# Attention stage of one transformer block: column-tiled products in 6 groups per four units instead of 14, reciprocals of 16 columns, VectorE's sums placed later

## The chip, the core and the metric

One core of one Trainium2 chip runs the whole program. Its engines work in parallel and wait for each other with semaphores: TensorE (PE, with its weight loads PEld), VectorE (DVE), ScalarE (ACT), GpSimd (POOL) and SyncE (SP), which here only starts transfers. The metric is the device time of one execution in microseconds (us).

## What is computed

A block of attention and a mixture of experts on x of 4 x 2048 x 512. Only the attention part and the shared expert run in the stage that changes:

```python
qkv = x @ Wqkv                       # x after a layer norm; 16 heads of 32
k, v = _compress(k, ...), _compress(v, ...)   # 2048 keys become 512, one null key is put ahead
dots = jnp.einsum('bhid,bhjd->bhij', q, k) * d ** (-0.5)
dots = jnp.where(mask, mask_value, dots)      # query i sees compressed key j if i >= 4j + 3
attn = jax.nn.softmax(dots, axis=-1)
out = jnp.einsum('bhij,bhjd->bhid', attn, v)
...
shared = jax.nn.silu(xf @ sh_gate_w) * (xf @ sh_up_w) @ sh_down_w
```

The block's output adds x, a Fourier transform of `out @ W_out + b_out`, `shared` and the routed experts. These other parts run in stages of their own, before and after.

## The kernel before

The program has stages one after the other: stage A (layer norm, projections, compression, routing), stage B (attention, shared expert, tables of the routing), then the routed experts and the transforms. The change touches only `stage_b`.

Stage B has NU = 64 units. A unit u is 512 queries (QC) of one batch for 4 heads (HPC), DH = 32 rows each. n = u % 4 (NCH = 4) says which quarter of the sequence it is: it sees n "past" blocks of 128 keys in full and one "diagonal" block under a mask. Each unit is cut into 12 slots k = 0..11 (SLOTS), written out in the same way on every engine. The slots are the order of the work; nothing but semaphores ties the engines together.

On PE a slot has six matmuls of the shared expert (`gate_up` in even units and the first four slots of odd ones, else `down`), then in slots 0 to 7 two `scores(u + 1, ...)` into the two banks `ps_s`, then the turned scores `scores_t` of this unit into the two banks `ps_t`, and last the column-tiled products. These use the array as four column tiles of 32, one for each head: `values` sums probabilities times values into `ps_o`, one call for each key block, and `denominators` sums the probabilities into `ps_d` with a matrix of ones. A call is four matmuls in the program and eight in the trace. I call calls that stand side by side with no other matmul between them a group. `pv_slots` puts the diagonal block in slot 6 and past block kt in slot 7 + 2 kt; `denominators` stands in slot 7 for n = 0 and otherwise in slot 0 of the next unit. For n = 0, 1, 2, 3 that is 2, 3, 4 and 5 groups, 14 in four units.

On DVE a slot has one or two steps of the shared expert (`gate_out`, `up_out`, `split_h`, `down_out`), in slot 1 `normalise(u - 1)`, in slots 2 to 5 a quarter each of the reciprocals of `den` (`invert`), in slots 0 to 7 two `row_max(u + 1, ...)`, which read `ps_s` and give the bank back, in slot 8 `negate`, and in slots 6, 8 and 10 the sums of the probabilities (`add_past`, for the n past blocks). `scores(i)` waits until `row_max(i - 2)` is done.

ACT takes the exponents of `ps_t` (`exponent`, `null_exponent`), the tanh of the gate and the rounded copies. POOL masks the diagonal block (`mask_diagonal`), scatters the routing table with single-column indirect DMAs (`scatter`, 10 or 11 in a unit while there are any) and multiplies `o` by the reciprocals (`finish`). `normalise(u)` waits for `finish(u - 1)` (`att_ready`). SP loads q, keys, values, x and its transpose, and stores `att` (`store_att`).

Of the kernel before, what the change touches and what calls it, by code (L numbers as in the profile page):

```python
# [11 lines left out]
ALU = mybir.AluOpType  # L12
# [3 lines left out]
P = 128  # L16
BATCH, SEQ, DIM = 4, 2048, 512
TOK = BATCH * SEQ
# [740 lines left out]
def stage_b(nc, t, early):  # L759
    ctx = ExitStack()  # L760
    with ctx:
# [14 lines left out]
        den = sb("den", [P, QC])  # L776
        o = sb("o", [P, QC])
# [60 lines left out]
        rden_ready = sem("rden_ready")  # L838
# [52 lines left out]

        def pv_slots(n, k):
            if k == 6:
                return [n]
            return [kt for kt in range(n) if 7 + 2 * kt == k]
# [29 lines left out]
        def _(sp):  # L925
# [85 lines left out]
            for u in range(NU):  # L1011
# [16 lines left out]
                if u:  # L1028
                    store_att(u - 1)
# [7 lines left out]
                if u in (NU // 2 - 2, NU // 2 - 1):  # L1037
                    load_raw(2 * u - NU + 12)
                    load_raw(2 * u - NU + 13)
            store_x(2 * NSTEP - 1)  # L1040
# [7 lines left out]
        def _(pool):  # L1048
            pool.iota(tokens[:, :], pattern=[[P, NTILE]], base=0, channel_multiplier=1).then_inc(tokens_ready, 1)

            def finish(u):

                pool.wait_ge(rden_ready, QTC * (u + 1))
                pool.wait_ge(od_emptied, u + 1)
                if u >= 2:
                    pool.wait_ge(att_out[u % 2], 16 * (u // 2))
                pool.tensor_tensor(att[u % 2][:, :], o[:, :], den[:, :], ALU.mult).then_inc(att_ready, 1)
# [14 lines left out]
            for u in range(NU):  # L1072
                mask_diagonal(u)
                g, part = (u - 1) // GU_UNITS - 1, (u - 1) % GU_UNITS
                mine = range(part * 4 * TOPK // GU_UNITS, (part + 1) * 4 * TOPK // GU_UNITS) if 0 <= g < NG else range(0)
                for i in mine[:4]:
                    scatter(g, i)
                if u:
                    finish(u - 1)
                for i in mine[4:]:  # L1080
                    scatter(g, i)
# [5 lines left out]
        def _(act):  # L1087
# [55 lines left out]

            split_w(0)
            max_rows(0)
            for u in range(NU):
                s, gate = steps(u)
                n = u % NCH
                for k in range(SLOTS):
# [18 lines left out]
                    for kt, h in t_slots(n, k):  # L1168
                        exponent(u, kt, h)
                    if u == 0 and k in (1, 3, 7):  # L1170
                        split_w((1, 3, 7).index(k) + 1)
# [8 lines left out]
        def _(dve):  # L1180
# [45 lines left out]
            def normalise(u):  # L1226
# [4 lines left out]
                if u:  # L1231
                    dve.wait_ge(att_ready, u)
                dve.tensor_tensor(den[:, :], ps_d[:, :], p_null[:, :], ALU.add).then_inc(den_ready, 1)
# [3 lines left out]
            def invert(u, i):  # L1237
                dve.wait_ge(den_ready, u + 1)
                part = den[:, i * P:(i + 1) * P]
                dve.reciprocal(part, part).then_inc(rden_ready, 1)  # L1240
# [102 lines left out]
            for u in range(NU):  # L1343
                s, gate = steps(u)
                for k in range(SLOTS):
# [30 lines left out]
                    if k == 1 and u:  # L1376
                        normalise(u - 1)
                    if 2 <= k < QTC + 2 and u:
                        invert(u - 1, k - 2)
# [14 lines left out]
                    if k in (6, 8, 10) and (k - 6) // 2 < u % NCH:  # L1394
                        add_past(u, (k - 6) // 2)
# [5 lines left out]
            normalise(NU - 1)  # L1401
            for i in range(QTC):
                invert(NU - 1, i)

        @block.tensor
        def _(pe):
# [64 lines left out]

            def gate_up(s, j, a, part):
# [47 lines left out]
            for u in range(NU):  # L1520
                s, gate = steps(u)
                n = u % NCH
                for k in range(SLOTS):
# [11 lines left out]
                    for kt in pv_slots(n, k):  # L1535
                        values(u, kt)
                    if k == 7 and n == 0:
                        denominators(u)
                    if k == 0 and u and (u - 1) % NCH:
                        denominators(u - 1)  # L1540
# [4 lines left out]
            denominators(NU - 1)  # L1545
# [767 lines left out]
def internal(nc):  # L2313

    def d(name, shape, dt=F32):
        return nc.dram_tensor(f"mid_{name}", shape, dt, kind="Internal").ap()
# [6 lines left out]
        attT=d("attT", (DC, P, TOK)), passed=nc.alloc_semaphore("passed"))  # L2323
# [81 lines left out]
```

## Time and profile before

| | |
|---|---|
| median of 3 runs | 5415.87 us (5412.05 to 5418.78) |
| the profiled execution's span, first to last instruction | 5418.5 us |
| PE busy | 5303.0 us, 98% |
| DVE busy | 3828.9 us, 71% |
| ACT busy | 2615.1 us, 48% |
| POOL busy | 3028.9 us, 56% |
| stage B | from about 710 to 2450 us of the span |

The execution that was profiled took what its span says; what lies around the span is not told apart, and the span is 2.6 us above the median of the runs. A share of busy time is a mean over stages with different limits. PE's matmuls are pipelined and their durations overlap, so that a busy PE may still lose time: what a matmul costs is read from the start of one to the start of the next.

### The profile page before, as it was taken

What the parts mean: (1) busy time and instruction counts of PE and PEld (TensorE: products, weight loads), DVE (VectorE), ACT (ScalarE), POOL (GpSimd) and SP (SyncE); (2) the same over time, 40 slices, a digit from 0 to 9 for tenths busy, and PEclk for the clock granted to TensorE, in tenths of its full rate; (3) what the DMA queues carried; (4) which work ended last, traced back from release to release, by engine and by line L of the source; (5) the groups of instructions that cost most, each with busy time, mean ns of one, the idle gap of its engine ahead of it and who ended that gap; (6) DMA issues with size and microseconds to landing.
All of it is one profiled execution on the core that took longest, in us unless ns stands there. A gap on an engine that the chain in (4) does not pass through costs nothing. (4 is left out here: it accounts for less than half of the span.)

```text
span 5418.5 us, 102292 instructions
## 1 busy us (share of the span) xinstructions
PE 5303.0 (98%) x32880; PEld 4440.9 (82%) x32880; DVE 3828.9 (71%) x7311; ACT 2615.1 (48%) x3833; POOL 3028.9 (56%) x2716
## 2 busy tenths in 40 slices
PE   8999989999999999998999999999999999999999
PEld 6888866766666667667999999989999999999786
DVE  6666667778787877775676666766667666666664
ACT  3333333333343333335666666666666666666410
POOL 1222215666666665115777777777777777777514
PEclk9999989999999999998999999999999999999999
DMA  7777764444454444435676677767787676676748
GB/s 239 248 242 255 250 173 129 133 134 119 136 148 135 119 141 118 134 98 119 134 158 112 134 170 150 163 132 167 158 227 158 135 164 129 134 156 113 178 154 289
DMA packets 500414, 864.75 MB, mean 160 GB/s; under 512 B 64388, under 2 KB 165493, under 8 KB 497694
## 3 DMA queue, kind: packets, MB, share of 16 engines
q1 hardware_dynamic: 356014, 567.12, 33.2%
q0 software_dynamic: 140928, 292.13, 29.5%
q10 hardware_dynamic: 3312, 3.47, 0.3%
q8 instruction: 88, 1.44, 0.1%
q14 instruction: 72, 0.59, 0.0%
HBM read 498.49 MB, written 330.47 MB: 153 GB/s over the span
## 5 line engine op out<-in xcount | busy, mean ns | idle before, releaser
L1754 POOL DMA_INDIRECT mid_base<-e_rows,e_ox x556 | 1160.3, 2087 | 372.5 <-POOL e_ox L1749 239.5
L1865 DVE TENSOR_TENSOR e_wgu_lo<-e_wgu,e_wgu_hi 128x2048 fp32r<-128x2048 f32 x278 | 637.5, 2293 | 806.4 <-ACT e_wgu_hi L1788 676.6
L1742 POOL DMA_INDIRECT e_xg<-mid_xn,e_ix x556 | 625.5, 1125 | 336.4 <-POOL e_ix L1739 226.4
L1801 ACT CAST e_xT_hi<-e_ps_t 128x512 fp32r<-128x512 f32 x556 | 299.1, 590 | 929.8 <-PE e_ps_t L1931 929.8
L1069 POOL DMA_INDIRECT mid_ids<-b_pairs,b_cell x512 | 614.3, 1200 | 141.8 <-issue 141.0
L1944 PE MATMUL e_ps_g<-e_xT_hi,e_wgu_hi 128*128 128x256 f32 x2224 | 652.9, 294 | 1.7 <-issue 1.7
L1944 PE MATMUL e_ps_g<-e_xT_lo,e_wgu_hi 128*128 128x256 f32 x2224 | 630.0, 283 | 0.0
L1944 PE MATMUL e_ps_g<-e_xT_hi,e_wgu_lo 128*128 128x256 f32 x2224 | 629.7, 283 | 0.0
L1944 PE MATMUL e_ps_u<-e_xT_hi,e_wgu_hi 128*128 128x256 f32 x2224 | 629.4, 283 | 0.0
L1944 PE MATMUL e_ps_u<-e_xT_lo,e_wgu_hi 128*128 128x256 f32 x2224 | 629.4, 283 | 0.0
L1944 PE MATMUL e_ps_u<-e_xT_hi,e_wgu_lo 128*128 128x256 f32 x2224 | 629.4, 283 | 0.0
L1197 DVE CUSTOM_DVE_ANT_0 b_ps_s<-b_ps_s,ab_mask,ab_s_null 128x32 f32<-128x32 f32 (+15 forms) x1024 | 460.3, 490 | 130.0 <-PE b_ps_s L1417 123.7
L1788 ACT CAST e_wgu_hi<-e_wgu 128x2048 fp32r<-128x2048 f32 x278 | 531.4, 1912 | 23.1 <-DMA e_wgu<-in_up_w 23.1
L1062 POOL TENSOR_SCALAR_AFFINE_SELECT b_p_diag<-b_p_diag 128x512 f32<-128x512 f32 x256 | 160.2, 650 | 537.4 <-ACT b_p_diag L1120 537.4
L1956 PE MATMUL e_ps_y<-e_wd_hi,e_hT_hi 128*128 128x512 f32 x1112 | 436.2, 392 | 0.0
L1956 PE MATMUL e_ps_y<-e_wd_lo,e_hT_hi 128*128 128x512 f32 x1112 | 436.0, 392 | 0.0
L1956 PE MATMUL e_ps_y<-e_wd_hi,e_hT_lo 128*128 128x512 f32 x1112 | 433.6, 390 | 0.0
L1944 PEld LDWEIGHTS e_ps_g<-e_xT_hi,e_wgu_hi 128*128 128x128 f32 x2224 | 426.4, 192 | 2.1 <-issue 2.1
L1944 PEld LDWEIGHTS e_ps_g<-e_xT_lo,e_wgu_hi 128*128 128x128 f32 x2224 | 427.9, 192 | 0.0
L1944 PEld LDWEIGHTS e_ps_u<-e_xT_lo,e_wgu_hi 128*128 128x128 f32 x2224 | 427.0, 192 | 0.0
L1944 PEld LDWEIGHTS e_ps_u<-e_xT_hi,e_wgu_lo 128*128 128x128 f32 x2224 | 427.0, 192 | 0.0
L1944 PEld LDWEIGHTS e_ps_g<-e_xT_hi,e_wgu_lo 128*128 128x128 f32 x2224 | 427.0, 192 | 0.0
(286 smaller groups left out, 13368.0 us busy)
## 6 DMA issues: line engine op xcount, KB each, us to landing
b_xT_hi<-mid_xT_hi SPq DMA_DIRECT2D x32, 1024.0 KB
b_xT_lo<-mid_xT_lo SPq DMA_DIRECT2D x32, 1024.0 KB
mid_base<-b_x SPq DMA_DIRECT2D x32, 1024.0 KB
e_wgu<-in_gate_w SPq DMA_DIRECT2D x62, 512.0 KB
e_wgu<-in_up_w SPq DMA_DIRECT2D x62, 512.0 KB
e_wd<-in_down_w SPq DMA_DIRECT2D x62, 512.0 KB
ec_cell<-mid_base SPq DMA_DIRECT2D x88, 256.0 KB, 4.9
ab_q<-mid_q_hi SPq DMA_DIRECT2D x82, 256.0 KB, 4.0
```

The costliest lines, as they stand in the source:

```text
L1062: pool.affine_select(p_diag[:, h, :], p_diag[:, h, :], [[1, QC]], ALU.is_ge, 0.0, base=1 - CF, channel_multiplier=-CF).then_inc(masked, 1)
L1069: pool.indirect_dma_start(t["ids"], bass.IndirectOffsetOnAxis(ap=cell[r][:, i:i + 1], axis=0), pairs[r][:, i, :], None).then_inc(scattered ...
L1197: dve.tensor_tensor_reduce(S[:, 0:w_], S[:, 0:w_], mask[:, NC - w_:NC], 1.0, null_of(u)[:, qt, h:h + 1], ALU.add, ALU.max, mx[:, qt, h:h + ...
L1742: pool.indirect_dma_start(xg[s][:, i, :], None, t["xn"], bass.IndirectOffsetOnAxis(ap=ix[s][:, i:i + 1], axis=0))\
L1754: pool.indirect_dma_start(t[f"base{i}"], bass.IndirectOffsetOnAxis(ap=ox[s][:, i:i + 1], axis=0), rows[s][:, i, :], None, compute_op=ALU.a ...
L1788: act.copy(wgu_hi[s][:, :], wgu[s][:, :]).then_inc(gu_hi_ready, 1)
L1801: act.copy(xT_hi[s][:, i * DC // 2 * RB:(i + 1) * DC // 2 * RB], ps_t[i][:, :]).then_inc(xT_hi_ready, 1)
L1865: dve.tensor_tensor(wgu_lo[s][:, :], wgu[s][:, :], wgu_hi[s][:, :].bitcast(F32), ALU.subtract)\
L1944: last = pe.matmul(dst[s][:, h * RB:(h + 1) * RB], w[s][:, w0:w0 + P], x[s][:, x0:x0 + RB], start=k == 0 and n == 0, stop=k == DC - 1 and ...
L1956: last = pe.matmul(ps_y[i][:, :], x[s][:, h0:h0 + P], w[s][:, h * DIM:(h + 1) * DIM], start=h == 0 and n == 0, stop=h == HC - 1 and n == 2)
```

## The change

`TILED` is a table that says for each n in which slot which `values` calls stand; `denominators` follows the last of them. The key SLOTS (12) stands for slot 0 of the next unit. The groups are now 1 for n = 0 (slot 7), 1 for n = 1 (slot 11), 2 for n = 2 (slot 11, and `denominators` alone in slot 0 of the next unit) and 2 for n = 3 (slot 6, and slot 0 of the next unit): 6 in four units. The number of calls is the same.

The four reciprocals of 128 x 128 on DVE become one of 128 x 16. Four rows of `den` (one for each head; the 32 rows of a head are equal) are spread over 128 partitions by a DMA (`turn_den`), inverted (`invert`), stored to DRAM (`store_rden`) and read back with each row repeated 32 times (`spread_rden`). ACT issues all three. The last unit keeps four reciprocals. `normalise` moves to slot 2 in units with n = 0, `invert` stands in slot 4 (5 for n = 0), and the sums go by the table `ADDS`. POOL issues 8 scatters ahead of `finish` in place of 4, and SP issues `store_att` behind its loads.

```diff
@@ -776,2 +776,4 @@
         den = sb("den", [P, QC])
+        den16 = sb("den16", [P, QC // DH])
+        rden = sb("rden", [P, QC])
         o = sb("o", [P, QC])
...
@@ -891,6 +896,8 @@
 
+        TILED = {0: {7: [0]}, 1: {11: [1, 0]}, 2: {11: [2, 0, 1], SLOTS: []}, 3: {6: [3, 0], SLOTS: [1, 2]}}
+
         def pv_slots(n, k):
-            if k == 6:
-                return [n]
-            return [kt for kt in range(n) if 7 + 2 * kt == k]
+            return TILED[n].get(k, [])
+
+        ADDS = {0: (), 1: (7,), 2: (8, 9), 3: (6, 8, 10)}
 
@@ -1027,4 +1034,2 @@
                     load_group(u // GU_UNITS + 1)
-                if u:
-                    store_att(u - 1)
                 if gate and s:
@@ -1039,2 +1044,4 @@
                     load_raw(2 * u - NU + 13)
+                if u:
+                    store_att(u - 1)
             store_x(2 * NSTEP - 1)
@@ -1052,3 +1059,3 @@
 
-                pool.wait_ge(rden_ready, QTC * (u + 1))
+                pool.wait_ge(rden_in, 16 * (u + 1))
                 pool.wait_ge(od_emptied, u + 1)
@@ -1056,3 +1063,3 @@
                     pool.wait_ge(att_out[u % 2], 16 * (u // 2))
-                pool.tensor_tensor(att[u % 2][:, :], o[:, :], den[:, :], ALU.mult).then_inc(att_ready, 1)
+                pool.tensor_tensor(att[u % 2][:, :], o[:, :], rden[:, :], ALU.mult).then_inc(att_ready, 1)
 
@@ -1075,3 +1082,3 @@
                 mine = range(part * 4 * TOPK // GU_UNITS, (part + 1) * 4 * TOPK // GU_UNITS) if 0 <= g < NG else range(0)
-                for i in mine[:4]:
+                for i in mine[:8]:
                     scatter(g, i)
@@ -1079,3 +1086,3 @@
                     finish(u - 1)
-                for i in mine[4:]:
+                for i in mine[8:]:
                     scatter(g, i)
@@ -1142,2 +1149,17 @@
                 act.copy(hT_hi[:, j, :], hT[:, :]).then_inc(h_hi_ready, 1)
+
+            def turn_den(u):
+
+                act.wait_ge(den_ready, u + 1)
+                act.dma_start(den16[:, :], den[0:P:DH, :].rearrange("h (j c) -> h j c", j=DH)).then_inc(den16_in, 16)
+
+            def store_rden(u):
+                act.wait_ge(den16_ready, u + 1)
+                act.dma_start(t["rden"].rearrange("h (j c) -> (h j) c", j=DH), den16[:, :]).then_inc(rden_out, 16)
+
+            def spread_rden(u):
+                act.wait_ge(rden_out, 16 * (u + 1))
+                if u:
+                    act.wait_ge(att_ready, u)
+                act.dma_start(rden[:, :], t["rden"][:, None, :].broadcast_to([HPC, DH, QC])).then_inc(rden_in, 16)
 
@@ -1169,2 +1191,8 @@
                         exponent(u, kt, h)
+                    if u and k == (3 if u % NCH == 0 else 2):
+                        turn_den(u - 1)
+                    if u and k == (6 if u % NCH == 0 else 5):
+                        store_rden(u - 1)
+                    if u and k == (8 if u % NCH == 0 else 7):
+                        spread_rden(u - 1)
                     if u == 0 and k in (1, 3, 7):
@@ -1232,2 +1260,3 @@
                     dve.wait_ge(att_ready, u)
+                    dve.wait_ge(den16_in, 16 * u)
                 dve.tensor_tensor(den[:, :], ps_d[:, :], p_null[:, :], ALU.add).then_inc(den_ready, 1)
@@ -1236,6 +1265,5 @@
 
-            def invert(u, i):
-                dve.wait_ge(den_ready, u + 1)
-                part = den[:, i * P:(i + 1) * P]
-                dve.reciprocal(part, part).then_inc(rden_ready, 1)
+            def invert(u):
+                dve.wait_ge(den16_in, 16 * (u + 1))
+                dve.reciprocal(den16[:, :], den16[:, :]).then_inc(den16_ready, 1)
 
@@ -1375,6 +1403,6 @@
                             down_out(s, k // 2 - 3 if k > 7 else 0)
-                    if k == 1 and u:
+                    if u and k == (2 if u % NCH == 0 else 1):
                         normalise(u - 1)
-                    if 2 <= k < QTC + 2 and u:
-                        invert(u - 1, k - 2)
+                    if u and k == (5 if u % NCH == 0 else 4):
+                        invert(u - 1)
                     if u + 1 < NU:
@@ -1393,4 +1421,4 @@
                         early.place_heads(dve, kc[1]).then_inc(heads_placed, 1)
-                    if k in (6, 8, 10) and (k - 6) // 2 < u % NCH:
-                        add_past(u, (k - 6) // 2)
+                    if k in ADDS[u % NCH]:
+                        add_past(u, ADDS[u % NCH].index(k))
                     g, part = (u - 1) // GU_UNITS, (u - 1) % GU_UNITS
@@ -1401,4 +1429,5 @@
             normalise(NU - 1)
+            dve.wait_ge(den_ready, NU)
             for i in range(QTC):
-                invert(NU - 1, i)
+                dve.reciprocal(rden[:, i * P:(i + 1) * P], den[:, i * P:(i + 1) * P]).then_inc(rden_in, 16 // QTC)
 
@@ -1470,2 +1499,9 @@
                 last.then_inc(d_filled, 1)
+
+            def tiled(u, k):
+                n = u % NCH
+                for kt in pv_slots(n, k):
+                    values(u, kt)
+                if k == max(TILED[n]):
+                    denominators(u)
 
@@ -1534,8 +1570,5 @@
                         scores_t(u, kt, h)
-                    for kt in pv_slots(n, k):
-                        values(u, kt)
-                    if k == 7 and n == 0:
-                        denominators(u)
-                    if k == 0 and u and (u - 1) % NCH:
-                        denominators(u - 1)
+                    if k == 0 and u:
+                        tiled(u - 1, SLOTS)
+                    tiled(u, k)
                     if k == 10:
@@ -1544,3 +1577,3 @@
                         scores_null(u)
-            denominators(NU - 1)
+            tiled(NU - 1, SLOTS)
 
...
```

PE, a unit with n = 0, from the scores of slot 6 to those of slot 7 and the groups that follow them (b_ps_f is the shared expert, b_ps_s the scores, b_ps_o `values`, b_ps_d `denominators`). Before:

```order
L1417 MATMUL b_ps_s<-ab_kc,ab_q 128x256 x2
L1456 MATMUL b_ps_o<-b_p_diag,ab_vc 32x512 x4
L1490 MATMUL b_ps_f<-b_xT_hi,b_wgu_hi 128x512
L1490 MATMUL b_ps_f<-b_xT_lo,b_wgu_hi 128x512
L1490 MATMUL b_ps_f<-b_xT_hi,b_wgu_lo 128x512
L1490 MATMUL b_ps_f<-b_xT_hi,b_wgu_hi 128x512
L1490 MATMUL b_ps_f<-b_xT_lo,b_wgu_hi 128x512
L1490 MATMUL b_ps_f<-b_xT_hi,b_wgu_lo 128x512
L1417 MATMUL b_ps_s<-ab_kc,ab_q 128x256 x2
L1469 MATMUL b_ps_d<-b_p_diag,b_ones 32x512 x4
L1490 MATMUL b_ps_f<-b_xT_hi,b_wgu_hi 128x512
```

And of the change:

```order
L1446 MATMUL b_ps_s<-ab_kc,ab_q 128x256 x2
L1526 MATMUL b_ps_f<-b_xT_hi,b_wgu_hi 128x512
L1526 MATMUL b_ps_f<-b_xT_lo,b_wgu_hi 128x512
L1526 MATMUL b_ps_f<-b_xT_hi,b_wgu_lo 128x512
L1526 MATMUL b_ps_f<-b_xT_hi,b_wgu_hi 128x512
L1526 MATMUL b_ps_f<-b_xT_lo,b_wgu_hi 128x512
L1526 MATMUL b_ps_f<-b_xT_hi,b_wgu_lo 128x512
L1446 MATMUL b_ps_s<-ab_kc,ab_q 128x256 x2
L1485 MATMUL b_ps_o<-b_p_diag,ab_vc 32x512 x4
L1498 MATMUL b_ps_d<-b_p_diag,b_ones 32x512 x4
L1526 MATMUL b_ps_f<-b_xT_hi,b_wgu_hi 128x512
```

What were two groups, with the six matmuls of the shared expert between them, is one group of both calls.

DVE, in a unit with n = 1, slots 3 and 4 (L1197 before and L1225 now is `row_max`; b_gated and b_hT are the shared expert; b_slot is the routing). Before:

```order
L1245 SCALAR_TENSOR_TENSOR b_gated<-b_gated,b_ps_f 128x512
L1240 RECIPROCAL b_den<-b_den 128x128
L1197 ISA b_ps_s,b_mx<-b_ps_s,ab_mask,ab_s_null 128x320
L1197 ISA b_mx 128x1
L1197 ISA b_ps_s,b_mx<-b_ps_s,ab_mask,ab_s_null 128x320
L1197 ISA b_mx 128x1
L1283 TENSOR_TENSOR b_slot<-b_slot,b_pos 128x256
L1253 SCALAR_TENSOR_TENSOR b_hT<-b_gated,b_ps_f 128x512
L1240 RECIPROCAL b_den<-b_den 128x128
```

And of the change:

```order
L1273 SCALAR_TENSOR_TENSOR b_gated<-b_gated,b_ps_f 128x512
L1225 ISA b_ps_s,b_mx<-b_ps_s,ab_mask,ab_s_null 128x320
L1225 ISA b_mx 128x1
L1225 ISA b_ps_s,b_mx<-b_ps_s,ab_mask,ab_s_null 128x320
L1225 ISA b_mx 128x1
L1311 TENSOR_TENSOR b_slot<-b_slot,b_pos 128x256
L1281 SCALAR_TENSOR_TENSOR b_hT<-b_gated,b_ps_f 128x512
L1268 RECIPROCAL b_den<-b_den 128x16
```

The two reciprocals of 128 columns of these slots are gone, and one of 16 columns stands in slot 4.

ACT, in a unit with n = 2, from its first exponents to the null exponent's copy (b_p_diag and b_p_past are exponents, b_gated the tanh, b_hT_hi a rounded copy). Before:

```order
L1120 ACTIVATE b_p_diag<-b_ps_t 128x512 x4
L1136 ACTIVATE b_gated<-b_ps_f 128x512
L1120 ACTIVATE b_p_past<-b_ps_t 128x512 x4
L1142 CAST b_hT_hi<-b_hT 128x512
L1120 ACTIVATE b_p_past<-b_ps_t 128x512 x2
L1136 ACTIVATE b_gated<-b_ps_f 128x512
L1120 ACTIVATE b_p_past<-b_ps_t 128x512 x2
L1142 CAST b_hT_hi<-b_hT 128x512
```

And of the change:

```order
L1127 ACTIVATE b_p_diag<-b_ps_t 128x512 x4
L1143 ACTIVATE b_gated<-b_ps_f 128x512
L1127 ACTIVATE b_p_past<-b_ps_t 128x512
L1154 DMA b_den<-b_den 128x1x16
L1127 ACTIVATE b_p_past<-b_ps_t 128x512 x3
L1149 CAST b_hT_hi<-b_hT 128x512
L1127 ACTIVATE b_p_past<-b_ps_t 128x512 x2
L1158 DMA mid_rden<-b_den 128x16
L1143 ACTIVATE b_gated<-b_ps_f 128x512
L1127 ACTIVATE b_p_past<-b_ps_t 128x512 x2
L1164 DMA b_rden<-mid_rden 128x1x512
L1149 CAST b_hT_hi<-b_hT 128x512
```

Three DMA issues stand among ACT's instructions; each has its wait for a semaphore ahead of it.

## Rows read from the trace of the kernel before

**Rows 1.** The page's part 1: busy us (share of the span) xinstructions.

```profile
PE 5303.0 (98%) x32880; PEld 4440.9 (82%) x32880; DVE 3828.9 (71%) x7311; ACT 2615.1 (48%) x3833; POOL 3028.9 (56%) x2716
```

**Rows 2.** By windows: PE, PEld, DVE, ACT, POOL busy, granted clock, DMA share, GB/s.

```profile
750.00:2448.00 1698.00, 1684.30 (x8246) 1171.22 (x8245) 1345.65 (x3473) 649.16 (x1020) 855.23 (x827) 1.00 0.44 127
```

**Rows 3.** Timeline of PE, `denominators` alone; start us, us, engine, line, out<-in.

```profile
1609.68 0.40 PE L1417 MATMUL b_ps_s<-ab_kc,ab_q 96*128 96x256 f32 x2
1610.02 1.07 PE L1469 MATMUL b_ps_d<-b_p_diag,b_ones 128*32 128x512 f32 x8
1611.01 0.50 PE L1490 MATMUL b_ps_f<-b_xT_hi,b_wgu_hi 128*128 128x512 f32 x1
1611.35 0.39 PE L1490 MATMUL b_ps_f<-b_xT_lo,b_wgu_hi 128*128 128x512 f32 x1
1611.57 0.39 PE L1490 MATMUL b_ps_f<-b_xT_hi,b_wgu_lo 128*128 128x512 f32 x1
```

**Rows 4.** Timeline, the stage's end, two calls side by side on PE.

```profile
2445.84 1.06 PE L1456 MATMUL b_ps_o<-b_p_past,b_vc 128*32 128x512 f32 x8
...
2446.72 1.04 PE L1469 MATMUL b_ps_d<-b_p_sum,b_ones 128*32 128x512 f32 x8
```

**Rows 5.** Timeline of PE, ends of slots 5 (n = 1, 2, 0).

```profile
1628.79 0.40 PE L1512 MATMUL b_ps_f<-b_wd_hi,b_hT_lo 128*128 128x512 f32 x1
1629.03 0.79 PE L1417 MATMUL b_ps_s<-ab_kc,ab_q 96*128 96x352 f32 x2
1630.02 0.47 PE L1512 MATMUL b_ps_f<-b_wd_hi,b_hT_hi 128*128 128x512 f32 x1 [0.21 <-DVE b_hT_lo L1257]
...
1656.12 0.49 PE L1417 MATMUL b_ps_s<-ab_kc,b_q 96*128 96x480 f32 x1 [0.24 <-DVE b_mx L1197]
1656.76 0.48 PE L1417 MATMUL b_ps_s<-ab_kc,b_q 96*128 96x480 f32 x1
...
1711.50 0.39 PE L1490 MATMUL b_ps_f<-b_xT_hi,b_wgu_lo 128*128 128x512 f32 x1
1711.99 0.74 PE L1417 MATMUL b_ps_s<-b_kc,ab_q 96*128 96x224 f32 x2
1712.57 0.40 PE L1490 MATMUL b_ps_f<-b_xT_hi,b_wgu_hi 128*128 128x512 f32 x1
```

**Rows 6.** Waits in stage B: who <- whom: us in total, times, longest.

```profile
PEld b_ps_s L1417 <- DVE b_mx L1197: 40.0, 102, 2.3
PE b_ps_s L1417 <- DVE b_mx L1197: 5.6, 19, 1.9
```

**Rows 7.** The view by lines, DVE and POOL in the same window.

```profile
L1240 DVE RECIPROCAL b_den<-b_den 128x128 f32<-128x128 f32 x252 | 238.3, 946 | 0.0
L1069 POOL DMA_INDIRECT mid_ids<-b_pairs,b_cell x512 | 614.3, 1200 | 141.8 <-issue 141.0
L1057 POOL TENSOR_TENSOR b_att<-b_o,b_den 128x512 f32<-128x512 f32 x63 | 83.2, 1320 | 187.7 <-DVE b_den L1240 171.1 <-issue 16.5
```

**Rows 8.** Timeline of DVE, a short reciprocal in stage A.

```profile
221.24 0.18 DVE L584 RECIPROCAL a_winv<-a_wsum 128x4 f32<-128x4 f32 x1
```

**Rows 9.** DMA issues: KB, us to landing; last row: q loads (L933).

```profile
mid_w<-a_w SPq DMA_DIRECT2D x16, 16.0 KB, 2.0
...
DMA to landing us min/median/max: 3.2/4.2/6.3
```

**Rows 10.** Timeline, a unit with n = 3, slots 2 to 5.

```profile
1678.86 0.60 ACT L1120 ACTIVATE b_p_past<-b_ps_t 128x512 f32<-128x512 f32 x1 [0.48 <-PE b_ps_t L1435]
...
1680.83 0.67 DVE L1253 SCALAR_TENSOR_TENSOR b_hT<-b_gated,b_ps_f 128x512 f32<-128x512 f32 x1
...
1683.92 0.32 PE L1417 MATMUL b_ps_s<-b_kc,ab_q 96*128 96x96 f32 x2
```

**Rows 11.** Timeline of ACT ahead of stage B, issues of transfers.

```profile
664.76 0.35 ACTq L128 DMA_DIRECT2D a_heads<-in_null_heads  x1
...
674.64 1.04 ACTq L145 DMA_DIRECT2D ab_raw<-in_sh_up  x1
```

More of the change, by code:

```diff
@@ L837, in stage_b @@
         od_emptied = sem("od_emptied")
-        rden_ready = sem("rden_ready")
+        den16_in = sem("den16_in")
+        den16_ready = sem("den16_ready")
+        rden_out = sem("rden_out")
+        rden_in = sem("rden_in")
         att_ready = sem("att_ready")
@@ L2322, in internal @@
         cnt=d("cnt", (P, EXPERTS)), ids=d("ids", (NSLOT, 2), I32), blk=d("blk", (1, 3 * P), I32), used=d("used", (1, 3), I32),
-        attT=d("attT", (DC, P, TOK)), passed=nc.alloc_semaphore("passed"))
+        attT=d("attT", (DC, P, TOK)), rden=d("rden", (HPC, QC)), passed=nc.alloc_semaphore("passed"))
 def layout(L0_attn_x, L0_attn_Wqkv, L0_attn_conv_w, L0_attn_conv_b, L0_attn_null_k, L0_attn_null_v, L0_attn_W_out,
```

## Prediction

> **What bounds the kernel now.** I read the shares of the whole span first (PE 98%, DVE 71% [rows 1]), then the stage's window, then PE's starts one by one. In the middle of stage B PE is busy 1684.30 of 1698.00 us at a granted clock of 1.00 (2.4 GHz), DVE 1345.65 (79%), ACT 649.16 (38%), POOL 855.23 (50%) [rows 2]. The window holds 63 units (POOL's product, which each unit has once, stands 63 times [rows 7]): 26.95 us a unit, 107.8 us for four. So the stage is PE's, and what leaves PE's row of starts leaves the time, as long as nobody makes PE wait. But busy does not mean fed. Two kinds of loss can be read in the starts.
>
> The first stands around each tiled group. A lone call of eight matmuls starts at 1610.02 and the next plain matmul at 1611.01, 0.99 us later; that plain matmul then takes 0.34 us to its successor where the following one takes 0.22 (1611.57 less 1611.35); and ahead of the group two score matmuls of 256 columns take 0.34 us (1609.68 to 1610.02), where 2 x 256 columns at 2.4 GHz are 0.21 [rows 3]. At the stage's end two calls stand side by side, and there the second starts 0.88 us after the first [rows 4].
>
> The second is DVE's lateness. Scores may run two banks ahead of `row_max`. In slot 5 of units with n = 1, 2 and 0 they catch up with it [rows 5]. n = 1: 352-column scores at 1629.03, next at 1630.02, 0.99 us for 0.29 of columns, 0.70 lost, the last part of it on `hT_lo`, also DVE's. n = 2: a wait of 0.24, then 0.64 for 0.20, 0.68 lost. n = 0: 0.49 for 0.22 and 0.58 for 0.19, 0.66 lost. That is 2.04 us in four units, and in just those slots DVE has inverted 3.8 us of reciprocals (946 ns each [rows 7]) beside its two `row_max`. The view of waits gives 40.0 + 5.6 us in all for the scores' wait on `row_max` [rows 6]; the 40.0 is the weight loader's idle, which partly lies under running matmuls.
>
> **Groups on PE.** The calls stay the same in number (10 of values and 4 of denominators in four units), 14 groups become 6, so 8 joins in four units, 16 x 8 = 128 joins. A join saves 0.99 - 0.88 = 0.11 at the end of the group, 0.34 - 0.22 = 0.12 at the first plain matmul, and 0.34 - 0.21 = 0.13 ahead of it. The last holds some of the small fixed cost that each short matmul has anyway (0.03, my estimate from 0.22 for 512 columns that are 0.21 of streaming, twice), so 0.33 in place of 0.36: 128 x 0.33 = 42 us. Bounds: in a burst of three or four calls the 0.88, seen once only, may not hold; at 0.99 for each call a join saves 0.22, 28 us. At the full 0.36 it is 46.
>
> **Reciprocals and sums on DVE.** Removed are 4 x 0.946 = 3.78 us a unit; added is one of 16 columns, between the 0.18 of a 4-column one [rows 8] and a quarter of 0.946. I take 0.2, so 3.6 us a unit go, all from slots 2 to 5. Lateness of 0.7 at slot 5 is well under 3.6, so it goes: 2.04 x 16 = 33 us. The sum of 2048 columns moves from slot 6 behind slot 7's or 8's `row_max` for n = 1 and 2, so it can't be what is late in its place; for n = 3 it stays, and that unit's `row_max` are the short ones. What is late next is PE itself. Bounds: 5.6 us if only PE's own row of waits counts, 46 us if the loader's row does too.
>
> The later sums don't hold up PE: for n = 2 slots 8 and 9 hold two sums, and the gate step of slot 11 comes behind them; PE meanwhile has four slots of six matmuls (5.4 us), the transposes and the null score, and a burst of three calls (3 x 0.88 + 0.33), about 9 us, against about 9 on DVE (the lag at slot 8, 0.7 + 0.8 + 4.6 + 0.7 + 0.7). That is even, and I put 0.1 to 0.2 us a cycle of four there.
>
> **Three transfers on ACT.** Each unit gets three issues on ACT, 0.35 to 1.04 us each [rows 11], 1.1 to 3 us a unit, and ACT has 16 us idle in each. Behind `turn_den` stand the exponents of slot 3, behind `store_rden` those of slot 6, behind `spread_rden` those of slot 8 (n = 3 alone). Each slot leaves ACT more than a microsecond, so 0.35 hides; the issue near 1.04 would delay an exponent by a few tenths, and PE's next turned score but one with it.
>
> The wait that counts is DVE's for `turn_den`, since two `row_max` stand behind it and PE behind these. In a unit with n = 3 [rows 10] the exponent of slot 2 ends at 1679.46, and the issue follows. DVE's `up_out` of slot 4 ends at 1681.50, `invert` would come then, and PE wants the bank of slot 4's first `row_max` at 1683.92. With 0.2 for the reciprocal and 0.5 to 0.75 for `row_max`, the data may land until about 1683.1: a landing of 3.7 us costs nothing. The kernel's 16 KB stores land in 2.0 us, its 256 KB loads of q in 3.2 to 6.3, 4.2 in the middle [rows 9]. `turn_den` moves 8 KB; I go by the nearest row, 2.0, with some excess from loads beside it (DMA is 44% busy [rows 2]). At 4.2 it would cost 0.5 us in each of 48 units (n = 0 has a slot more), 24 us; at 6.3, 2.6 x 48 = 125 us. I put 5 us for the units in which a large transfer is in the way, together with the burst above.
>
> POOL's `finish` now comes behind 8 scatters. With its pauses one takes (614.3 + 141.8) / 512 = 1.48 us [rows 7], so 8 take 11.8 us behind the masks, done some 17 us into a unit; the third transfer is issued in slot 7 or 8, at 15 to 19 us. `normalise` of the next unit waits for this product, DVE and PE behind it. Tightest is n = 0: from the issue to slot 1 of the next unit there are five slots of at least 1.36 us, some 1.2 us of scores and transposes, and ACT is about 1.6 ahead: 9.6 us, less the product's 1.32, so 8.3 us for the landing. A q load of the same 256 KB landed within 6.3, so I cost it at nothing.
>
> A page speaks against this. The Trainium skill, "DMA: Bandwidth & Descriptors", section "Why a DMA increments its semaphore by 16 and not by 1", says that a transfer is spread over the largest number of engines, up to 16, that divides the slowest dimension on both sides; four rows would then get 4 of 16. No row here shows it.
>
> SP's `store_att` goes behind the loads of x and its transpose: these are issued earlier, nothing waits longer for them, and it saves nothing either, since PE never stands on them in the view of waits.
>
> **Sum.** -42 - 33 + 5 = -70 us. The profiled span of 5418.5 becomes 5348.5; the median of the runs lies 2.6 below the span, so 5346. All of it should stand in stage B, the other stages are unchanged.
>
> **Rivals.**
> (1) Another wait takes DVE's place. For it: ACT's exponents for the third past block now wait in slot 7 for the sum of slot 6, and bursts of 3 us keep the turned scores from ACT. Against: DVE falls to some 17.5 of 25.9 us. The gain would be the joins alone less a few: 35 to 45 us, 5376.
> (2) More is gained: every wait that goes back to DVE vanishes (46 in place of 33 [rows 6]) and `hT_lo` and gate steps come earlier by as much again as half of that: 42 + 46 + 7 = 95, 5321.
> (3) The spread transfer is slow as a mechanism of its own: if only four engines carry it, its 256 KB take four times the 2.2 us by which a q load exceeds a small one (4.2 - 2.0), 2.0 + 8.8 = 10.8 us. The tightest unit is then 2.5 us late, 16 x 2.5 = 40 us, and the time 5386. The page above is the rule for it. Against: no row shows a transfer from four rows.
> (4) Slower than before: `turn_den` lands late, because it queues behind the x and transpose loads of 1 MB that `store_att` no longer holds back. It decides from a landing of 3.7 + 75/48 = 5.3 us on, where the gain of 75 is gone; at 6.3 [rows 9] it is -75 + 125, 5466.
> (5) The joins save only 28 and the reciprocals 6, the lower ends together: 5384.
>
> **Chances.** Forecast 0.57 (its own range 5332 to 5362), (1) 0.15, (2) 0.10, (3) 0.06, (4) 0.06, (5) 0.06. The range of 8 in 10 takes in the forecast, most of (1) and (2) and part of (3) and (5): 5322 to 5388. A measurement of this kernel tells 0.2%, 11 us, from no change. Faster takes in all but (4) and a few mixed cases: 0.91, the same 0.04, slower 0.05.
>
> **What would show it.** In stage B's window the unit falls from 26.95 to about 25.85 us. Starts inside a burst are 0.88 us a call apart, and 96 groups are left. The scores' wait for `row_max` falls under 10 us and slot 5 costs what slot 4 does. DVE's wait for `turn_den`'s data and its wait for POOL's product are rare. Wrong would be: DVE idle ahead of the 16-column reciprocal by more than a microsecond as a rule (4), or ahead of `normalise` on `b_att` (3), PE's turned scores waiting for ACT (1), or calls in a burst 0.99 apart (5).

## The result and the profile after

| | before | after |
|---|---|---|
| median of 4 runs, same chip | 5416.51 us (5412.05 to 5418.78) | 5379.33 us (5374.19 to 5383.16) |
| the profiled execution: its time, its span | 5418.78, 5418.5 | 5374.19, 5372.4 |

The ratio after to before is 0.9929, 95% interval 0.9917 to 0.9941: 0.7% faster, 37 us where I had forecast 70. The time is inside the range, and outside the forecast's own range (5332 to 5362). One execution of the kernel before, among the comparisons for the second four experiments below, took 6459.85 us at a granted clock of 0.751 and is in no ratio.

Page of the kernel after, part 1, busy us (share of the span) xinstructions, in answer to [rows 1]:

```profile
PE 5240.4 (98%) x32880; PEld 4454.3 (83%) x32880; DVE 3667.2 (68%) x7122; ACT 2606.9 (49%) x3833; POOL 2988.5 (56%) x2716
```

Windows, stage B, in answer to [rows 2]; it holds 63 units again (POOL's product below), in 1659 us where it was 1698:

```profile
750.00:2409.00 1659.00, 1622.88 (x8231) 1185.57 (x8229) 1176.45 (x3285) 647.62 (x1017) 816.61 (x825) 1.00 0.48 141
```

A unit is 26.33 us after 26.95. DVE fell from 79% to 71%, as the removed reciprocals say. But PE is now busy 97.8% of the window, after 99.2%: it stands idle for 36 us of it where it was 14, and that is the sign of the missing half.

Groups by lines in the same window (us in all, ns of one | idle before, and for whom), in answer to [rows 7]:

```profile
L1064 POOL TENSOR_TENSOR b_att<-b_o,b_rden 128x512 f32<-128x512 f32 x63 | 119.2, 1892 | 470.0 <-DMA b_rden<-mid_rden 470.0
...
L1268 DVE RECIPROCAL b_den<-b_den 128x16 f32<-128x16 f32 x63 | 15.6, 248 | 29.0 <-DMA b_den<-b_den 28.9
```

The short reciprocal takes 248 ns (I took 0.2). POOL's product waits 7.5 us a unit for the third transfer, and no row of waits shows anyone standing behind it for that. One product takes 1892 ns where it took 1320 ([rows 7]); more on that under n = 2. DVE, though, waits 28.9 us for the first.

What was forecast for PE's joins stands in PE's timeline, the burst at the end of a unit with n = 1, in answer to [rows 3, 4]: calls start 0.88 and 0.86 us apart, the next plain matmul comes 0.98 after the last call, and only the first and the last matmul of the burst pay the entry and the exit.

```profile
1719.53 0.40 PE L1548 MATMUL b_ps_f<-b_wd_hi,b_hT_lo 128*128 128x512 f32 x1
1719.85 1.06 PE L1485 MATMUL b_ps_o<-b_p_diag,b_vc 128*32 128x512 f32 x8
1720.73 1.04 PE L1485 MATMUL b_ps_o<-b_p_past,b_vc 128*32 128x512 f32 x8
1721.59 1.04 PE L1498 MATMUL b_ps_d<-b_p_sum,b_ones 128*32 128x512 f32 x8
1722.57 0.50 PE L1526 MATMUL b_ps_f<-b_xT_hi,b_wgu_hi 128*128 128x512 f32 x1
1722.90 0.40 PE L1526 MATMUL b_ps_f<-b_xT_lo,b_wgu_hi 128*128 128x512 f32 x1
```

The same slot 5 of n = 1 that lost 0.70 in [rows 5] now has scores at 1708.26 and the next matmul at 1708.58, 0.32 us for 352 columns:

```profile
1708.26 0.49 PE L1446 MATMUL b_ps_s<-b_kc,b_q 96*128 96x352 f32 x2
1708.58 0.42 PE L1548 MATMUL b_ps_f<-b_wd_hi,b_hT_hi 128*128 128x512 f32 x1
```

And these are the waits of stage B after (who <- whom: us, times, longest), in answer to [rows 6]; the two of b_ps_s are that group's, the rest are new or were small:

```profile
DVE b_den L1268 <- DMA b_den<-b_den: 28.9, 18, 4.6
PEld b_ps_f L1548 <- DVE b_x L1292: 25.7, 30, 1.4
PEld b_ps_s L1446 <- DVE b_mx L1225: 24.5, 50, 3.5
PEld b_ps_f L1526 <- DVE b_gated L1273: 22.0, 17, 2.2
...
PE b_ps_f L1548 <- DVE b_x L1292: 14.1, 16, 0.9
...
PE b_ps_s L1446 <- DVE b_mx L1225: 9.2, 9, 3.1
PE b_ps_f L1526 <- DVE b_gated L1273: 7.0, 16, 1.3
```

Counts of 16 to 18 are once in four units. There are three places.

**n = 0, slots 5 and 6.** DVE stands 1.38 us ahead of the 16-column reciprocal, with two `row_max` behind it, and PE catches up with them. `turn_den` was issued at 1679.34 and its data was there at 1685.62, 6.3 us later. Timeline of SP's and ACT's issues and of DVE:

```profile
1675.55 0.31 SPq L949 DMA_DIRECT2D ab_kc<-mid_kc_hi  x1
1675.90 0.43 SPq L949 DMA_DIRECT2D ab_kc<-mid_kc_lo  x1
1676.38 0.43 SPq L949 DMA_DIRECT2D ab_kc<-mid_kc_hi  x1
1676.85 1.14 SPq L952 DMA_DIRECT2D ab_vc<-mid_vc  x1
...
1679.34 0.54 ACTq L1154 DMA_DIRECT2D b_den<-b_den  x1
...
1685.62 0.25 DVE L1268 RECIPROCAL b_den<-b_den 128x16 f32<-128x16 f32 x1 [1.38 <-DMA b_den<-b_den]
```

Windows, the stretch in which `turn_den` is issued; the last column but one says that all DMA engines are full (share 1.05):

```profile
1674.00:1683.00 9.00, 9.00 (x56) 6.17 (x49) 4.60 (x17) 2.05 (x4) 6.07 (x9) 1.00 1.05 241
```

The keys and values of the next batch (L949, L952) are loaded as soon as the last `values` of the batch before has read the old ones, and the change moved that call into slot 0, here at 1673.52 to 1675.26, right ahead of `turn_den`.

**n = 1, slot 9.** The sum moved to slot 7 stands ahead of `down_out(1)` on DVE, which empties the bank that slot 9's `down` fills. PE's last matmul is at 1714.95, the next at 1716.20, 1.25 us in place of 0.23. Timeline:

```profile
1713.26 2.29 DVE L1251 TENSOR_TENSOR b_p_sum<-b_p_diag,b_p_past 128x2048 f32<-128x2048 f32 x1
...
1714.95 0.39 PE L1548 MATMUL b_ps_f<-b_wd_hi,b_hT_lo 128*128 128x512 f32 x1
1715.46 0.69 DVE L1292 TENSOR_TENSOR b_x<-b_ps_f,b_x 128x512 f32<-128x512 f32 x1
...
1716.20 0.50 PE L1548 MATMUL b_ps_f<-b_wd_hi,b_hT_hi 128*128 128x512 f32 x1 [0.87 <-DVE b_x L1292]
```

**n = 2, end of slot 11.** Two sums run one behind the other from 1742.47, the second 3.20 us long; the gate step behind them ends at 1749.35, and PE, which has finished its burst, waits for it:

```profile
1742.47 2.29 DVE L1251 TENSOR_TENSOR b_p_sum<-b_p_diag,b_p_past 128x2048 f32<-128x2048 f32 x1
...
1743.71 2.19 POOL L1064 TENSOR_TENSOR b_att<-b_o,b_rden 128x512 f32<-128x512 f32 x1 [4.35 <-DMA b_rden<-mid_rden]
...
1744.86 3.20 DVE L1251 TENSOR_TENSOR b_p_sum<-b_p_sum,b_p_past 128x2048 f32<-128x2048 f32 x1
...
1748.67 0.68 DVE L1273 SCALAR_TENSOR_TENSOR b_gated<-b_gated,b_ps_f 128x512 f32<-128x512 f32 x1
```

Why is the second sum longer than the first? POOL's product is what goes with it. In all 16 units with n = 2 the product ends 3.4 us after the first sum's start, whether it began 0.56 or 1.71 us after it, so it seems held until the first sum is done; it then reaches 1.05 us into the second sum, and this one takes 3.2 us. A cast of 16 x 2048 on ACT runs there too, but such a cast lies 1.1 to 1.3 us under the sums of n = 3 as well, and these take 2.28. Where the second sum comes later (sum2_11 below) it takes 2.28 too. No run moved the product alone.

To add this up I took PE's starts of 56 units (4 to 59) in each trace and split each slot into the columns at 2.4 GHz, 0.88 a call and 0.33 a group, and the rest, in which PE stands; a remainder of about 0.1 us a slot that all kernels share is taken off. The table is my working on the traces; it has the slots in which a kernel stands over 0.3 us, in us a unit, and what four units take:

| kernel | n=0: 5, 6 | n=1: 5, 7, 8, 9 | n=2: 5, 7, 8, 9, 11 | four units |
|---|---|---|---|---|
| before | 0.70, 0 | 0.79, 0, 0.1, 0 | 0.79, 0.1, 0.1, -0.1, 0 | 107.5 |
| after | 0, 1.01 | 0, 0.2, 0.1, 1.05 | 0.1, 0.1, 0, 0, 0.38 | 105.2 |
| joins | 0.70, 0.1 | 0.79, 2.19, 0.61, 0.65 | 0.80, 2.14, 0.72, 0.42, -0.1 | 111.9 |
| sums_old | 0, 0.83 | 0, 2.42, 0.34, 0.30 | 0.1, 2.11, 0.54, 0.87, -0.1 | 109.7 |
| recips | 0, 0 | 0, 0.1, 0.1, 0 | 0.49, 0, 0.1, -0.1, 0.1 | 105.3 |
| all_inv | 0, 0 | 0, 0.2, 0.1, 0 | 0.44, 0, 0, 0, -0.1 | 103.0 |

Slot 5's three losses are gone but for 0.1, some 2.2 us in four units. In their place come 1.0 (n = 0), 1.0 (n = 1) and 0.5 (n = 2; 0.38 above -0.14, which is what slot 11 shows where nothing waits), 2.5 us, 16 x 2.5 = 40 us.

### The profile page after: what moved, and what is told of

It is laid out like the page before. It is cut to its first block and busy times, and to the rows that moved or that the text cites. A ratio compares the mean times of both kernels' runs of the same rounds, so it can differ in the third digit from the quotient of the medians.

```text
span 5372.4 us, 102355 instructions
## 1 busy us (share of the span) xinstructions
PE 5240.4 (98%) x32880; PEld 4454.3 (83%) x32880; DVE 3667.2 (68%) x7122; ACT 2606.9 (49%) x3833; POOL 2988.5 (56%) x2716
## 5 line engine op out<-in xcount | busy, mean ns | idle before, releaser
L1787 POOL DMA_INDIRECT mid_base<-e_rows,e_ox x556 | 1179.3, 2121 | 371.6 <-POOL e_ox L1782 261.5
L1225 DVE CUSTOM_DVE_ANT_0 b_ps_s<-b_ps_s,ab_mask,ab_s_null 128x32 f32<-128x32 f32 (+15 forms) x1024 | 474.5, 505 | 310.4 <-PE b_ps_s L1446 305.3
L1076 POOL DMA_INDIRECT mid_ids<-b_pairs,b_cell x512 | 542.2, 1059 | 142.0 <-issue 141.0
L1977 PEld LDWEIGHTS e_ps_u<-e_xT_hi,e_wgu_hi 128*128 128x128 f32 x2224 | 427.0, 192 | 0.0
```

The source lines that it names most:

```text
L1076: pool.indirect_dma_start(t["ids"], bass.IndirectOffsetOnAxis(ap=cell[r][:, i:i + 1], axis=0), pairs[r][:, i, :], None).then_inc(scattered ...
L1225: dve.tensor_tensor_reduce(S[:, 0:w_], S[:, 0:w_], mask[:, NC - w_:NC], 1.0, null_of(u)[:, qt, h:h + 1], ALU.add, ALU.max, mx[:, qt, h:h + ...
L1787: pool.indirect_dma_start(t[f"base{i}"], bass.IndirectOffsetOnAxis(ap=ox[s][:, i:i + 1], axis=0), rows[s][:, i, :], None, compute_op=ALU.a ...
L1977: last = pe.matmul(dst[s][:, h * RB:(h + 1) * RB], w[s][:, w0:w0 + P], x[s][:, x0:x0 + RB], start=k == 0 and n == 0, stop=k == DC - 1 and ...
```

## The experiments

All times are medians of 4 runs; the kernel before had 5415.0 us on the chip of the first four, 5418.2 on that of the next four and 5418.5 on that of the last two. A difference of two kernels below is one of medians; the 95% intervals of the ratios reach 7 to 9 us to either side, so the smaller differences lean on the table above as much as on the clock.

**joins.** The kernel before with the groups of the kernel after alone (`TILED`, `tiled`); reciprocals, sums and transfers are as before.

```diff
+        TILED = {0: {7: [0]}, 1: {11: [1, 0]}, 2: {11: [2, 0, 1], SLOTS: []}, 3: {6: [3, 0], SLOTS: [1, 2]}}
...
-                    for kt in pv_slots(n, k):
-                        values(u, kt)
-                    if k == 7 and n == 0:
-                        denominators(u)
-                    if k == 0 and u and (u - 1) % NCH:
-                        denominators(u - 1)
+                    if k == 0 and u:
+                        tiled(u - 1, SLOTS)
+                    tiled(u, k)
```

> The kernel before with the 6 groups alone; reciprocals of 128 columns and the sums stay where they were. Theory: the joins take 42 us off PE, but slots 6 and 7 of n = 1 and 2 lose the 1.2 us groups under which DVE worked off a sum of 2.3 us and its lateness, so PE stands there 1.5 to 2 us a unit more (some 3.5 in four units, 56 us): 5416 - 42 + 56, about 5430, between 5400 and 5440. Rival, the joins are worth their 42 us whatever DVE does: 5374.

Measured 5491.27, ratio 1.0137 [1.0120, 1.0154]: slower than before, and slower than either number. Its waits in stage B:

```profile
PE b_ps_f L1519 <- DVE b_x L1264: 30.2, 15, 2.1
PE b_ps_f L1497 <- DVE b_gated L1245: 28.4, 15, 2.4
```

Joining takes two groups (2 x 1.21 us of PE's work) out of slots 6 and 7 of n = 1 and n = 2, and this had been the cover of the sum in slot 6. Without it PE stands 2.2 us in slot 7 of both. The waits are not all: over the stage 78 us in this trace are at half the clock (see sums_old), by my count some 39 us of PE's work.

**sums_old.** The kernel after with the sums where they were.

```diff
-        ADDS = {0: (), 1: (7,), 2: (8, 9), 3: (6, 8, 10)}
+        ADDS = {0: (), 1: (6,), 2: (6, 8), 3: (6, 8, 10)}
```

> The kernel after, with the sums back in the slots in which they stood before (slot 6 for n = 1, slots 6 and 8 for n = 2). With the groups joined and the old reciprocals (joins) PE stood 2.1 us in slot 7 of n = 1 and of n = 2. Theory: the sum in slot 6 is the cause, a DVE step of more than 2 us ahead of slot 7's row_max; the short reciprocals take off only the 0.8 us by which DVE was late in slot 5, so some 1.3 us stay in slot 7 of both, while the sum is no longer ahead of down_out(1) (1.04 us in n = 1) and only one is left near slot 11 of n = 2 (0.3 to 0.5): 16 x (2.6 - 1.5) = +18 us on the kernel after's 5379, 5397 (5390 to 5405). Rival: it was the long reciprocals' lateness that turned into the 2.1 us; with short ones the sum in slot 6 is free, slot 7 costs nothing, and the two waits at the units' ends go: 16 x 1.5 = 24 us less, 5355.

Measured 5452.65, ratio 1.0064 [1.0048, 1.0081]: the theory's place and sign, four times its size. Two things were wrong in my number. The short reciprocals take nothing off slot 7: DVE had already caught up with PE and waited for slot 6's scores, and the sum stands behind that slot's `row_max`, however early DVE is itself. Timeline, a unit with n = 1:

```profile
1751.88 0.63 DVE L1225 CUSTOM_DVE_ANT_0 b_ps_s<-b_ps_s,ab_mask,ab_s_null 128x384 f32<-128x384 f32 x1 [0.60 <-PE b_ps_s L1446]
...
1752.96 2.29 DVE L1251 TENSOR_TENSOR b_p_sum<-b_p_diag,b_p_past 128x2048 f32<-128x2048 f32 x1
...
1753.23 0.51 PE L1446 MATMUL b_ps_s<-b_kc,b_q 96*128 96x384 f32 x2
...
1755.30 0.67 DVE L1292 TENSOR_TENSOR b_x<-b_ps_f,b_x 128x512 f32<-128x512 f32 x1
...
1756.03 0.50 PE L1548 MATMUL b_ps_f<-b_wd_hi,b_hT_hi 128*128 128x512 f32 x1 [2.29 <-DVE b_x L1292]
```

And the clock gives way. In the unit after this one (n = 2) PE stands again, for 1.85 us from 1782.7, and a microsecond after it has started once more, matmuls of 512 columns start 0.43 us apart instead of 0.23, eight of them. Windows (the granted clock is the last column but two), the whole stage, the stretch behind the 2.29 us of n = 1, and these:

```profile
750.00:2409.00 1659.00, 1589.43 (x7922) 1164.93 (x7920) 1128.71 (x3204) 624.50 (x979) 800.99 (x816) 0.98 0.47 138
...
1758.00:1762.00 4.00, 4.00 (x21) 3.33 (x20) 1.06 (x4) 1.11 (x1) 2.65 (x3) 1.00 0.18 69
...
1780.00:1785.00 5.00, 3.15 (x14) 2.27 (x13) 4.84 (x8) 1.09 (x2) 1.62 (x2) 1.00 0.15 52
...
1786.00:1789.00 3.00, 3.00 (x9) 2.35 (x8) 2.97 (x7) 0.62 (x1) 2.54 (x3) 0.50 0.23 88
```

0.50 is the lower of the two levels, 1.2 GHz. Over the stage it is 0.98, where before and after have 1.00 ([rows 2] and the window above). It doesn't fall after every such wait: behind the 2.29 us of n = 1 it stayed at 1.00. By my count of the trace 61 us of the stage are at the lower clock, some 31 us of PE's work, and the part of slots 8 and 9 in the table is mostly this. So the sums' move, which I had priced at nothing, is worth 73 us once the groups are joined, some 31 of them the clock's, and joins less sums_old, 38.6 us, is the reciprocals' (with a part of the clock in it, 39 less 31).

**recips.** The kernel after with the 14 groups and the old sums: the reciprocals and transfers without the joins. It also has the change's other edits: `normalise` in slot 2 for n = 0, the 8 scatters, and `store_att` behind the loads. No run parts these from the reciprocals.

> The changed kernel with the 14 groups and the sums of slots 6 and 8 as before, so the short reciprocal with its three transfers alone. Theory: the slot 5 waits of 2.04 us in four units go (-33), and in n = 0 the late landing of the turned sums costs 0.9 us (+14): 5397, with DVE idle ahead of the short reciprocal in n = 0 units as in the changed kernel. Rival, the landing costs nothing where slot 6 has a group behind it: 5384. Other rival, the short reciprocals gave nothing: 5416.

Measured 5384.33, ratio 0.9941 [0.9924, 0.9957]: 31 us less than before, the rival's number. The reciprocal still comes 5.1 to 6.4 us after `turn_den`'s issue in units with n = 0, and DVE waits 0.3 to 0.9 us for it in 10 of the 15, but PE's slot 6 shows nothing. A group stands there on PE, between slot 6 and slot 7; the landing is also about 1 us earlier than in the kernel after, and no run parts the two. Only 0.49 in slot 5 of n = 2 stays, where DVE again waits for `turn_den`:

```profile
DVE b_den L1268 <- DMA b_den<-b_den: 23.6, 28, 1.8
...
PE b_ps_s L1446 <- DVE b_mx L1225: 5.1, 12, 2.1
```

**sum1_8, sum2_11.** The kernel after, with one sum moved in each.

```diff
-        ADDS = {0: (), 1: (7,), 2: (8, 9), 3: (6, 8, 10)}
+        ADDS = {0: (), 1: (8,), 2: (8, 9), 3: (6, 8, 10)}    # sum1_8
+        ADDS = {0: (), 1: (7,), 2: (8, 11), 3: (6, 8, 10)}   # sum2_11
```

> The changed kernel with the sum of n = 1 in slot 8 behind down_out(1) in place of slot 7 ahead of it. Theory: the 1.04 us that PE stands at the end of slot 9 in every n = 1 unit goes, 16 x 1.04 = 16.6 us: 5363. Rival, that wait has another cause (the copy of x or POOL's port), or DVE is late for the next step instead: 5379, no change.

> The changed kernel with the second sum of n = 2 in slot 11, behind the gate step, in place of slot 9 ahead of it. Theory: the 0.52 us that PE stands behind the burst of slot 11 goes, 16 x 0.52 = 8 us: 5371. Rival, the denominators of slot 0 now wait for this sum: PE gains nothing or loses up to 1 us a unit, 5379 to 5395.

Measured 5364.58 (5363.06 to 5369.69), 14.8 below the kernel after, and 5370.47 (5358.74 to 5371.6), 8.9 below it. In sum1_8 slot 9 of n = 1 shows 0.01, in sum2_11 slot 11 of n = 2 shows -0.14. Both as the theory has it.

**kv_later, inv0_6.** Two ways to be rid of the wait in n = 0: the load of keys and values goes to the units with n = 1, or the inversion and the store go one slot later.

```diff
-                if u % NCH == 0 and u // NCH + 1 < ITEMS:
+                if u % NCH == 1 and u // NCH + 1 < ITEMS:    # kv_later
```

```diff
-                    if u and k == (5 if u % NCH == 0 else 4):
+                    if u and k == (6 if u % NCH == 0 else 4):    # inv0_6, DVE
                         invert(u - 1)
...
-                    if u and k == (6 if u % NCH == 0 else 5):
+                    if u and k == (7 if u % NCH == 0 else 5):    # inv0_6, ACT
                         store_rden(u - 1)
```

> The changed kernel with the loads of keys and values issued one unit later, in units with n = 1 in place of n = 0. Theory: turn_den lands 6 to 7 us after its issue in n = 0 because these 1 MB of loads, held until the values of slot 0 are done, and the stored x are in the DMA engines; without them it lands within 4.5 us, DVE doesn't idle there, and PE's 0.93 us at the end of slot 6 go, 16 x 0.93 = 15 us: 5364. In n = 1 nothing else is loaded at that time, and turn_den of slot 2 may lose up to 0.3 us. Rival, the landing is as slow because of the order of the rows or the store of x alone: 5379, DVE idle as before.

> The changed kernel with invert in slot 6 (and store_rden in slot 7) of units with n = 0, in place of 5 and 6. Theory: DVE arrives 1.6 us later, after the usual landing of 6.3 us: PE's wait shrinks from 0.93 to under 0.2 us, 12 us off, 5367. Rival, the wait only moves one slot on, since POOL's product then comes late for normalise of the next unit: 5379 or more.

Measured 5364.23 (5356.29 to 5367.63), 15.1 below the kernel after, and 5369.1 (5366.21 to 5370.1), 10.2 below it. The same unit as above in kv_later, `turn_den` and the reciprocal, now without a wait:

```profile
1673.91 0.54 ACTq L1154 DMA_DIRECT2D b_den<-b_den  x1
...
1678.67 0.24 DVE L1268 RECIPROCAL b_den<-b_den 128x16 f32<-128x16 f32 x1
```

That is 4.76 us from the issue, and the reciprocal did not wait: 14 of the 15 units with n = 0 have 4.7 to 4.8, the other 5.9. In the kernel after, 13 have 5.9 to 7.8, the first has 9.5, and the last, behind which no keys are left to load, 4.76. The window of 9 us around this issue has a DMA share of 0.69:

```profile
1668.91:1677.91 9.00, 9.00 (x55) 6.35 (x48) 4.79 (x17) 1.83 (x5) 6.08 (x9) 1.00 0.69 202
```

So it is the loads of keys and values that hold up the 8 KB, and DVE's wait for these is what costs PE a microsecond: scores' waits for `row_max` fall to

```profile
PEld b_ps_s L1446 <- DVE b_mx L1225: 9.3, 18, 2.6
...
PE b_ps_s L1446 <- DVE b_mx L1225: 3.3, 5, 2.1
```

which is near the "under 10 us" that the prediction had expected of the change.

**all_inv, all_kv, best.** The two sums together (slot 8 for n = 1; 8 and 11 for n = 2) with inv0_6, with kv_later, and with both.

> The changed kernel with the sum of n = 1 in slot 8, the second sum of n = 2 in slot 11, and invert in slot 6 of n = 0. Theory: the three waits are independent, and their gains add: 5379 - 16 - 8 - 12 = 5343. Rival, one takes the other's place (the unit is held by DVE's order somewhere else): above 5355.

> The changed kernel with the sum of n = 1 in slot 8, the second sum of n = 2 in slot 11, and the loads of keys and values one unit later. Theory, all three waits gone: 5379 - 16 - 8 - 15 = 5340, and the stage's unit 25.5 us. Rival: above 5355.

> The kernel after with all four edits: sums in slot 8 (n = 1) and in 8 and 11 (n = 2), the inversion for n = 0 in slot 6 and the store in 7, and load_kv in units with n = 1. Theory: the inversion's later slot and the later loads cure the same wait of n = 0, so together they bring no more than one alone: all_inv has 5343 and all_kv 5344, with 0.1 to 0.2 us a cycle more in slots 7 (n = 0) or 3 (n = 1) in the one than in the other, so 5341 (5338 to 5345). Rival: the two waits were only partly cured by each (the loads still delay other transfers, the slot still moves the third one), and together they bring 5 us or more: 5338 or less.

Measured 5343.09 (5341.6 to 5345.96), ratio 0.9864 [0.9847, 0.9882]; 5344.18 (5340.72 to 5346.26), 0.9865 [0.9847, 0.9882]; and 5343.48 (5340.79 to 5354.34), 0.9859 [0.9843, 0.9876]. The parts add up (14.8 + 8.9 + 10.2 = 34, measured 36; with kv_later's 15.1 it would be 39, measured 35), and the second repair of n = 0 brings nothing beside the first. All three are faster than the kernel after; what they still lose is 0.44 to 0.57 in slot 5 of n = 2, where DVE waits 0.3 to 1.5 us for `turn_den` in most units. In the kernel after this is 0.1, so it grew as the other waits went; why, no run shows.

## Why the prediction was right, and where it was not

**Groups on PE** (-42): right. The pitch in a burst is 0.88. By the clock of the runs: recips has all but the joins, and with the joins and their three waits repaired (all_inv) it is 5384.33 - 5343.09 = 41 us faster. The 0.33 a join is so borne out by the whole, not term by term.

**Reciprocals** (-33): right, with the small edits that recips shares. 31 us from before to recips, 38.6 from joins to sums_old; slot 5 of n = 0, 1 and 2 stands in none of the kernels with the short reciprocal, but for what `turn_den` itself costs n = 2. The sum of both terms, -75, on the 5418.2 that the kernel before had beside all_inv, is 5343, and all_inv measured 5343.09.

**The step that failed is the +5** "together with the burst above". It measured 36 (after less all_inv), in three parts of which I had one at the wrong size and two at nothing. That the time is still inside the range is in part luck: none of the rivals that gave the range its upper end was one of these three waits.

1. "n = 0 has a slot more", and so I took the 48 other units for the ones at risk. They had their data in time nearly always (the reciprocal stands 3.1 to 4.3 us behind the issue in n = 1, 3.4 to 4.6 in n = 2 and 2.0 to 2.8 in n = 3, with a wait in 5 of the 48). In n = 0 DVE comes 4.76 us after the issue (kv_later), and the landing took 6 to 7.7 behind the loads of keys and values. These are issued 3.8 us ahead of `turn_den` in the kernel after and 5.9 in recips, so the joined group moved them up to it. I had looked at SP's reorder of x and `store_att`, and not at what the keys' load waits for. 10 to 15 us (inv0_6, kv_later).
2. "The later sums don't hold up PE": I compared DVE and PE over the stretch for n = 2 (9 us each, "even") and gave it 0.1 to 0.2 us. It is 0.5, and nine tenths of a microsecond of DVE's time there I had not counted: the second sum took 3.20 us where I had 2.3, with POOL's product across its start. 9 us (sum2_11).
3. For n = 1 I asked only what stands behind the sum among the `row_max`, and not that `down_out(1)` does, for whose bank PE is ready 1.9 us after the sum's start (1713.26, 1715.18). 15 us (sum1_8).

That the move of the sums is needed at all was not in the prediction either. It priced both terms separately and added them; joins and sums_old show that they do not stand alone: without the sums' move the joins lose 75 us with the long reciprocals (joins against before) and 68 with the short ones (sums_old against recips) instead of bringing 42.

**The rivals.** (1) had the number, 5376, by the wrong road: it had the turned scores wait for ACT, and PE's rows of waits have none for them; another wait did take DVE's place, and it was DVE's own. (2) did not come: 24.5 us of the loader's row stayed. (3): the condition holds and the price does not, see below. (4) came for one unit in four, through other loads than I had named; in the other 48 units, where the prediction's own sum made a landing of 6.3 us cost 125 us, it did not come. (5) is excluded by the pitch.

On (3), two views of the kernel after, windows (1714.20 to 1717.40) and DMA packets (1714.10 to 1717.70), of a stretch in which the spread is the only transfer; it was issued at 1712.80, and its product starts at 1717.97:

```profile
1714.20:1717.40 3.20, 2.33 (x11) 1.62 (x10) 3.17 (x9) 0.00 (x0) 0.00 (x0) 1.00 0.23 80
...
DMA packets 132, 0.26 MB, mean 73 GB/s; under 512 B 4, under 2 KB 4, under 8 KB 132
```

A share of 0.23 is 3.7 of 16 engines, and beside 128 packets of data there are 4 small ones, where by my count of the trace the six transfers of SP around 1675 leave 96, 16 each. So the rule that rival (3) took from the Trainium skill, "DMA: Bandwidth & Descriptors", section "Why a DMA increments its semaphore by 16 and not by 1", agrees with this trace: four engines carried it. What failed is the price of 10.8 us. The packets took 3.3 us, and the product starts 4.6 to 5.4 us after the issue in most units and at most 7.6, inside the 8.3 us that were free. By these packets 16 engines would need 0.8 us for 256 KB (3.3 x 4 / 16, my estimate), so the 2.2 us that I took times four was for the most part not the time of 16 engines at work.

## What to carry to other kernels

When work is taken off the bounding engine, list for each place what it had been covering: here 2.4 us of matmuls hid a vector step of 2.3 us, and by where that step stands the same joins, on the kernel with short reciprocals, make it 68 us slower (recips to sums_old) or 41 us faster (recips to all_inv). A large step on a helper engine is to be placed by what stands behind it in its own queue and by when the bounding engine wants that, not by whether the engine has room on average. And a small transfer on which an engine waits is to be placed by what other queues issue in the microseconds before it; what those issues wait for moves with the edit too.

## What I had not expected of the hardware

- 8 KB issued on ACT while the keys' and values' loads fill the DMA engines (share 1.05) take 6.0 to 7.7 us to be there, and in 14 of 15 units at most 4.77 with those loads moved away (share 0.69); the 16 KB stores in stage A took 2.0 in the middle [rows 9].
- PE's granted clock fell to 0.50 for some 3 us after PE had stood 1.85 us and run again for one, and did not after a stand of 2.29 us in the same trace. In the kernel after, whose waits in stage B are mostly of 1 us, it stays 1.00. So a wait on PE can cost more than itself: in sums_old slots 8 and 9 of n = 2 lost 1.4 us more behind the 2.1 of slot 7.
- The reciprocal's time follows its columns: 0.18 us for 4 [rows 8], 0.248 for 16, 0.946 for 128 [rows 7].
- DVE's sum of 128 x 2048 and POOL's product of 128 x 512 hold each other up. The product takes 1.32 us before and 1.89 after, 2.19 in the row above; the second of two sums that stand side by side takes 3.20 us in place of 2.29 where the product reaches across its start. This is read from the traces; no run moved the product alone.
